# ViT layers on one core: in each MLP pair the transpositions move behind the first output tile, on DVE the normalised rows come first, on POOL the deviation comes ahead of the bias

## The reference

```python
for i in range(DEPTH):                      # DEPTH 4, DIM 128, HID 256, HEADS 8
    y = layernorm(h, ln1_w[i], ln1_b[i])
    ...                                     # attention
    h = h + (o @ proj_w[i] + proj_b[i])
    y = layernorm(h, ln2_w[i], ln2_b[i])
    y = jax.nn.gelu(y @ fc1_w[i] + fc1_b[i], approximate=False)
    h = h + (y @ fc2_w[i] + fc2_b[i])
```

## Time and profile before

| | us |
|---|---|
| median of 3 runs | 4164.19 |
| the profiled execution | 4193.22 |
| its span, which the profile shows | 4191.4 |
| mean granted TensorE clock | 0.943 of full speed |
| PE busy | 3591.3 (86%) |
| DVE, ACT, POOL busy | 2534.1, 1868.7, 2256.9 |
| time of PE's idle before L502, put down to the copy L605 | 58.5 |

### The profile page before, as it was taken

The page is one execution under the profiler, slowest core; times in us unless marked ns, Lnnn a source line. Parts: engine busy times, 40 slices in busy tenths (PEclk is TensorE's granted clock), DMA queues, the critical chain, the costliest instruction groups (busy, mean ns, idle before and its releaser), DMA issues. The chain is left out here.

```text
span 4191.4 us, 92430 instructions
## 1 busy us (share of the span) xinstructions
PE 3591.3 (86%) x30906; PEld 2764.9 (66%) x30906; DVE 2534.1 (60%) x6578; ACT 1868.7 (45%) x3340; POOL 2256.9 (54%) x2633
## 2 busy tenths in 40 slices
PE   8779999879999879999878999886887887876973
PEld 8757777667777657777656777763333665655763
DVE  1246776557776546777546777555775887865211
ACT  0036666336666435666534666542332443311331
POOL 0065663566664466666365666354554663264776
PEclk9879999999999989999998999998999998997997
DMA  6556664036666025666114666300000223131342
GB/s 222 162 106 122 126 127 92 3 72 127 125 125 117 8 53 109 123 126 127 37 36 89 122 126 125 72 1 28 22 22 20 57 64 48 35 87 41 65 63 29
DMA packets 456034, 341.81 MB, mean 82 GB/s; under 512 B 70659, under 2 KB 440171, under 8 KB 455595
## 3 DMA queue, kind: packets, MB, share of 16 engines
q1 hardware_dynamic: 413635, 314.62, 36.4%
q0 software_dynamic: 27136, 16.42, 2.9%
q10 hardware_dynamic: 15008, 7.51, 0.7%
HBM read 227.69 MB, written 109.29 MB: 80 GB/s over the span
## 5 line engine op out<-in xcount | busy, mean ns | idle before, releaser
L720 DVE TENSOR_REDUCE a_neg_max<-a_S 99x4 f32<-99x788 f32 x1024 | 1003.7, 980 | 560.3 <-PE a_S L351 546.5
L533 ACT ACTIVATE a_probs<-a_St 99x792 f32<-99x792 f32 (+1 forms) x1024 | 850.3, 830 | 683.5 <-PE a_St L368 671.9
L368 PE MATMUL a_St<-a_q_st,a_k_st 99*99 99x198 bf16 (+1 forms) x4096 | 530.1, 252 | 84.4 <-DMA a_q_st<-a_max_rows 70.2
L351 PE MATMUL a_S<-a_k_st,a_q_st 96*99 96x197 bf16 x4096 | 551.9, 258 | 45.7 <-DVE a_neg_max L720 45.5
L351 PEld LDWEIGHTS a_S<-a_k_st,a_q_st 96*99 96x99 bf16 x4096 | 399.5, 128 | 266.8 <-DVE a_neg_max L720 221.5
L368 PEld LDWEIGHTS a_St<-a_q_st,a_k_st 99*99 99x99 bf16 (+1 forms) x4096 | 391.5, 126 | 116.7 <-DMA a_q_st<-a_max_rows 69.6
L385 PE MATMUL a_O<-a_probs,a_v_aug 99*32 99x198 f32 (+1 forms) x8192 | 464.5, 339 | 0.4
L663 POOL TENSOR_TENSOR h<-h,a_rows 99x512 f32<-99x512 f32 x128 | 162.5, 1270 | 277.3 <-DVE a_m_xn L801 277.3
L385 PEld LDWEIGHTS a_O<-a_probs,a_v_aug 99*32 99x32 f32 (+1 forms) x8192 | 246.6, 110 | 84.7 <-issue 2.1
L631 POOL CAST a_max_parts<-a_neg_max 99x32 bf16<-99x32 f32 x128 | 26.8, 209 | 471.8 <-DVE a_neg_max L720 471.8
L512 PEld LDWEIGHTS a_O<-a_w,a_gelu 128*99 128x99 f32 x2048 | 241.7, 168 | 45.5 <-issue 29.2
(11 more groups left out here) (267 smaller groups left out, 7473.8 us busy)
## 6 DMA issues: line engine op xcount, KB each, us to landing
xpatch<-in_x SPq DMA_DIRECT2D x64, 594.0 KB, 3.7
spill_q<-a_parts SPq DMA_DIRECT2D x384, 99.0 KB
spill_k<-a_parts SPq DMA_DIRECT2D x384, 99.0 KB
a_k_st<-spill_k SPq DMA_DIRECT2D x128, 297.0 KB
a_q_st<-spill_q SPq DMA_DIRECT2D x128, 297.0 KB
a_k_st<-spill_k SPq DMA_DIRECT2D x128, 198.0 KB
a_q_st<-spill_q SPq DMA_DIRECT2D x128, 198.0 KB
a_k_st<-spill_k SPq DMA_DIRECT2D x128, 99.0 KB
```

The costliest lines, as they stand in the source:

```text
L351: mm = nc.tensor.matmul(S[0:TC, j // 2, j % 2 * TB:j % 2 * TB + NTOK], q_st[p % 4][0:SPLIT, head, b * TB + c * TC:b * TB + (c + 1) * TC], ...
L368: mm = nc.tensor.matmul(St[0:keys, j // 2, j % 2 * TB:(j % 2 + 1) * TB], k_st[p][:, head, first:first + keys], q_st[p][:, head, b * TB:(b ...
L533: nc.scalar.activation(probs[0:keys, u % 4, :].rearrange("p (x t) -> p x t", x=2), St[0:keys, :, 0:2 * TB], ACT.Exp).then_inc(s["probs"], 1)
L720: nc.vector.tensor_reduce(out.rearrange("p (x y) -> p x y", x=2), S[0:TC, :, 0:2 * TB].rearrange("p x (y t) -> p x y t", y=2)[:, :, :, 0:N ...
```

## The change

PE: the second layer's four output tiles get a helper `down(t)`; the first tile is issued, then the transpositions of pair k + 2, then the other three tiles. DVE: normalised rows (k + 2) are made ahead of the statistics (k + 3). POOL: the deviation (k + 3) is made ahead of the bias (k + 2). No instruction is added or dropped and no wait changes its value.

```diff
@@ tensor, mlp
+                    def down(t):
+                        for h in range(2):
+                            mm = nc.tensor.matmul(O[0:TC, t * D:(t + 1) * D], gl[k % 2][:, h, t * TC:(t + 1) * TC],
+                                                  m.w2[:, h * D:(h + 1) * D], start=(h == 0), stop=(h == 1))
+                        return mm
...
                         wait(pe, s["m_gelu"], 2 * (n + 1))
                         wait(pe, s["m_h"], n)
-                        for t in range(4):
-                            for h in range(2):
-                                mm = nc.tensor.matmul(O[0:TC, t * D:(t + 1) * D], gl[n % 2][:, h, t * TC:(t + 1) * TC],
-                                                      m.w2[:, h * D:(h + 1) * D], start=(h == 0), stop=(h == 1))
-                        mm.then_inc(s["m_fc2"], 1)
+                        down(0)
                     if 0 <= k + 2 < PAIRS:
...
                         mm.then_inc(s["m_turned"], 1)
+                    if 0 <= k < PAIRS:
+                        for t in range(1, 3):
+                            down(t)
+                        down(3).then_inc(s["m_fc2"], 1)
@@ gpsimd, mlp: this block moves from the head of the function to its end
-                    if 0 <= k + 2 < PAIRS:
-                        n = at(l, k + 2)
-                        wait(pool, s["m_xn"], n + 1)
-                        hp = g.h[0:TC, (k + 2) * 4:(k + 3) * 4, :]
-                        nc.gpsimd.tensor_tensor(hp, hp, m.b2.unsqueeze(1).to_broadcast([TC, 4, D]),
-                                                ALU.add).then_inc(s["m_bias"], 1)
@@ vector, mlp: this block moves from the head of the function to behind m_xn
-                    if 0 <= k + 3 < PAIRS:
-                        n = at(l, k + 3)
-                        q = n % 2
-                        wait(dve, s["h_done"], n + 1)
-                        wait(dve, s["m_aggr"], n - 1)
-                        for t in range(4):
-                            op = nc.vector.bn_stats(m_stats[q][:, t, :], g.h[0:TC, (k + 3) * 4 + t, :])
-                        op.then_inc(s["m_stats"], 1)
```

More of the change, by code:

```diff
@@ L509, in mlp @@
                         wait(pe, s["m_h"], n)
-                        for t in range(4):
-                            for h in range(2):
-                                mm = nc.tensor.matmul(O[0:TC, t * D:(t + 1) * D], gl[n % 2][:, h, t * TC:(t + 1) * TC],
-                                                      m.w2[:, h * D:(h + 1) * D], start=(h == 0), stop=(h == 1))
-                        mm.then_inc(s["m_fc2"], 1)
+                        down(0)
                     if 0 <= k + 2 < PAIRS:
-                        n = at(l, k + 2)
-                        wait(pe, s["m_xn"], n + 1)
-                        wait(pe, s["m_yT"], n)
+                        n2 = at(l, k + 2)
+                        wait(pe, s["m_xn"], n2 + 1)
+                        wait(pe, s["m_yT"], n2)
                         wait(pe, s["yT"], at(l + 1, done + 6))
@@ L676, in mlp @@
                                                 ALU.pow).then_inc(s["m_rstd"], 1)
+                    if 0 <= k + 2 < PAIRS:
+                        n = at(l, k + 2)
+                        wait(pool, s["m_xn"], n + 1)
+                        hp = g.h[0:TC, (k + 2) * 4:(k + 3) * 4, :]
+                        nc.gpsimd.tensor_tensor(hp, hp, m.b2.unsqueeze(1).to_broadcast([TC, 4, D]),
+                                                ALU.add).then_inc(s["m_bias"], 1)
                 program(lambda l, k: None, attn, mlp, looped=False)(pool)
@@ L788, in mlp @@
                 def mlp(l, k, done):
+                    if 0 <= k + 2 < PAIRS:
+                        n = at(l, k + 2)
+                        wait(dve, s["m_rstd"], n + 1)
+                        wait(dve, s["m_turned"], n - 1)
+                        nc.vector.tensor_tensor(m_xn[n % 2][:], g.h[0:TC, (k + 2) * 4:(k + 3) * 4, :],
+                                                m_rstd[n % 2][:].to_broadcast([TC, 4, D]), ALU.mult).then_inc(s["m_xn"], 1)
                     if 0 <= k + 3 < PAIRS:
@@ L796, in mlp @@
                         op.then_inc(s["m_stats"], 1)
[L797 to L802, removed]
                     if 0 <= k + 3 < PAIRS:
```

3 lines of the change are left out of this document (1 added, 2 removed).

## The result

The change makes the kernel slower by half a per cent: 4196.1 us (median of 20 runs, 4182.7 to 4216.4) against 4178.1 us (20 runs, 4154.1 to 4194.3), a ratio of 1.0053 with a 95% interval of 1.0038 to 1.0069. The forecast was 4189.0 against 4164.2, +25 us; the medians lie 18 us apart, and the ratio says 16 to 29 us.

What follows compares the result with a forecast made beforehand. The prediction took PE, busy 86% of the span, as the bound. Layer 3 (+1), the other three layers (+21) and the clock (+3) gave +25 us on 4164: 4189 us, 0.6% slower, range 4140 to 4214.

Steps and rivals of the forecast that it cites:

- The plain pair: MLP pairs without an attention step: POOL's bias holds `m_xn`, so the period is 4.35 us against 4.28, 0.07 worse.
- X + 3.22: Plain pair: when POOL starts the bias, counted from X, the moment `m_xn` of a pair really begins (us).
- X + 3.28: Plain pair: earliest start of the next `m_xn` on DVE, counted from the real beginning of this pair's `m_xn` (us).
- an instruction that slips in first: Plain pairs: DVE's `m_xn` gets ahead of POOL's bias and is not held; pairs take 3.53, total 4117 us; chance 0.12.
- the mixture: Plain pairs: `m_xn` is held by the bias in some pairs only; total 4135 to 4165 us; chance 0.06.
- The upper bound: Plain pair with nothing else late: PE alone takes 1.43 + 1.75 + 0.35 = 3.53 us, 0.75 less than now.
- Layer 3 and the first 13 intervals: Layer 3's 30 intervals: +1 us; layers 0 to 2 up to their first attention step: +0.8 us a layer.
- The wait in the steps: Attention steps: the bias ahead of `xn` makes PE wait longer, 4.4 us idle instead of 2.5; +2.6 four times a layer.
- The clock: Behind the attention steps: nine of twelve already show a clock fall, the other three fall too, about 1 us each: +3.
- From step to step: Between attention steps, some loss returns: behind k = 21 the cycle takes 25.25 us, today 23.6, so +1.7, not +2.6.
- The sum: Whole kernel: 1 for layer 3, 21 for the three other layers, 3 for the clock, together +25 us.
- The slower rival: Twelve attention steps cost 1.6 us more each (second clock fall 1.2, L616 held 0.44): 4209 us; chance 0.14.

Runs made afterwards that it cites:

- e5: Changed kernel with POOL's bias replaced by a memset of a scratch tile of about the same length, output bias left out; 4136.4 us (1 run).
- e6: Changed kernel with POOL's bias replaced by the same tensor_tensor on scratch tiles, output bias left out; 4203.4 us (1 run).
- e8: Changed kernel with POOL's bias split into two instructions of two row blocks each; 4179.7 us (1 run).
- e1: Changed kernel with only POOL's order undone (bias ahead of deviation again), PE and DVE as changed; 4107.7 us (5 runs), ratio 0.9861 to the original.
- e11: Original kernel with POOL making the attention step's xn ahead of pair k's bias and deviation; 4122.4 us (6 runs), ratio 0.9903 to the original.
- e12: Changed kernel with POOL making the attention step's xn ahead of pair k's deviation and bias; 4132.9 us (1 run).
- e10: e1 with POOL also making the attention step's xn ahead of pair k's bias and deviation; 4066.5 us (5 runs), ratio 0.9784 to the original.
- e7: Changed kernel with POOL's bias moved behind the attention step's xn, in the steps behind k = 13, 17, 21, 25, 29 only; 4205.8 us (1 run).
- e4: Original kernel with DVE's and POOL's new orders only, PE's order as before; 4179.0 us (1 run).

## Why the prediction was right, and where it was off

**The plain pair.** Forecast 4.35, measured 4.36. `m_xn` starts 0.06 behind the bias, as worked out from X + 3.22 and X + 3.28, and ends where the bias's shown end less 0.14 lets it: 2772.43 + 1.27 - 0.14 + 0.67 = 2774.23, measured 2774.24. e5, e6 and e8 show the mechanism, e1 its price. The rival of an instruction that slips in first falls, and so does the mixture. (That rival's price has a slip: 3 x (-16 + 6) is -30 and not -28, which makes it 4115; nothing hangs on it.) By the Trainium skill (SBUF — State Buffer, section "Who interferes with whom") a DVE instruction with two SBUF inputs contends with a GpSimd instruction that reads SBUF and not with one that only writes it, and the issue order decides who blocks; e5 and e6 agree with that, with 0.68 beside a memset and 1.76 beside a reader.

**The upper bound.** I had 3.53 for PE alone; e1 shows 3.42. What was off is the 1.43 from first to second layer, read where PE had just been idle. With no idle time ahead, the second layer starts 1.33 behind (2771.65 to 2772.98, and 1.33 in e1 too, 29 of the 30 times in layer 3; the one that follows a wait is 1.43). So the harm of POOL's order was larger than I said: 0.94 a pair and not 0.82.

**Layer 3 and the first 13 intervals.** Forecast +1 and +0.8; measured +1.3, and +0.7 in each layer (59.24 to 59.91 from the first layer of pair 0 to that of pair 14).

**The wait in the steps.** Forecast: transpositions of `xn` 8.76 behind the last first layer, 4.4 idle; measured 8.83 and 4.31. Over twelve steps the forecast +1.9 each is 22.8, and the rows give 51.7 - 30.2 = 21.5. The steps are the larger part of the loss, as forecast. PE's account of the MLP stages bears it out: its idle time rose by 25.1 (119.9 to 145.0), 21.5 of it ahead of the transpositions of `xn`, and its busy time by 4.8. Removing the wait on both sides (e11, e12) takes only 12 of the 30 us away, because a part of it comes back ahead of the transpositions of `m_xn`, in the changed order alone.

**The clock.** This is the term that was mis-sized: 3 us taken, about 10 found. Stretches of 8 us from the step's resumption on, before the change, behind k = 17 and 21 of layer 0 and the same two of layer 1 (columns as before):

```profile
831.54:839.54 8.00, 7.17 (x22) 4.23 (x23) 0.78 (x5) 2.27 (x4) 6.35 (x5) 0.59 0.11 28
856.07:864.07 8.00, 6.58 (x40) 4.81 (x40) 0.98 (x6) 2.87 (x5) 7.39 (x6) 1.00 0.17 48
1487.43:1495.43 8.00, 6.58 (x35) 4.57 (x36) 2.25 (x10) 2.81 (x6) 7.10 (x6) 1.00 0.15 41
1509.92:1517.92 8.00, 6.58 (x19) 3.92 (x20) 0.78 (x5) 1.69 (x3) 6.97 (x6) 0.54 0.14 38
```

After the change, behind k = 21 of layer 0:

```profile
856.09:864.09 8.00, 6.58 (x18) 4.11 (x19) 0.00 (x0) 1.69 (x3) 5.91 (x5) 0.50 0.11 29
```

1.00 is the upper level (2.4 GHz), 0.50 the lower (1.2 GHz). Before, nine of the twelve steps behind k = 13 to 25 show a fall, after all twelve, as forecast. But before has, without any change of order, the same stretch with and without a fall, and that gives the price. From the first layer of pair 18 to that of pair 22 it took 24.53, 22.47 and 24.63 in layers 0, 1 and 2, the 22.47 being the one at 1.00: 2.1 a fall. From pair 22 to pair 26 it took 23.45, 27.67 and 23.45, the 27.67 being the one at 0.54: 4.2 a fall. In after the three steps that were spared fall too: 4.2 + 2.1 + 4.2 = 10.5, an estimate at the prices of before. PE's busy time gives the same size for all falls together: in layers 0 to 2 it rose from 551.0 - 113.3 = 437.7 to 555.9 - 111.9 = 444.0 (+6.3), while in layer 3, where nothing falls, the new order took 1.5 off it; 6.3 + 3 x 1.5 = 10.8. I had multiplied a mean clock over 4 us and taken about 1 us; at 0.50 over 8 us it is 4, and the work under it is on the path. Whether the fall is tied to PE's idle time was argued in the prediction and is shown by the steps without it: of the twelve rows of 8 us, twelve are at 1.00 in e12, eleven in e11 and ten in e10 (the rest 0.79, 0.78 and 0.76), none in e1, which still idles 39.9 in all. In the 8 us behind these, all twelve are at 1.00 in e11, and five are below it in e12 and in e10 each, where PE has new waits of up to 4.4 us for `m_xn`; e11 has none of these.

**From step to step.** By the prediction behind k = 21 the next step resumes 25.25 later; it is 28.19 (856.09 to 884.28). The 23.6 that it started from is a cycle of before without a fall (856.07 to 879.53 is 23.46). The rows of after say where the other 2.9 are. The first layer comes 7.18 behind the resumption (863.27) and not 4.53, with PE at the lower clock: 2.65. The three pairs behind it take 4.56, 3.42 and 4.20 (to 875.45), 12.18 together, where the forecast comes to 11.96, and the wait ends 8.83 behind the last first layer, where it had 8.76. So this fall costs 2.7 and not the 4.2 of the same length of fall in before. There the first layer came 2.0 later (1509.92 to 1516.49, 6.57) and the pair behind it took 2.2 more; in after that pair was to wait for `m_xn` by the forecast, and what PE lost by the clock went into this wait.

| first layer to first layer, layers 0, 1, 2 | before | after |
|---|---|---|
| pair 0 to 14 | 59.24, 59.24, 59.24 | 59.91, 59.90, 59.91 |
| 14 to 18 | 22.53, 22.54, 22.54 | 24.05, 24.79, 23.97 |
| 18 to 22 | 24.53, 22.47, 24.63 | 26.46, 26.62, 26.41 |
| 22 to 26 | 23.45, 27.67, 23.45 | 28.19, 28.49, 28.18 |
| 26 to 30 | 31.10, 31.31, 31.16 | 31.42, 31.57, 31.41 |
| 30 to 31 | 17.42, 18.38, 18.38 | 18.56, 19.47, 18.58 |

**The sum.** Forecast 1 + 21 + 3 = 25. Measured in the MLP stages of the two profiled executions: 1.3 in layer 3, 2.0 in the first 14 intervals of the three others, 10.5 for the falls by the working above, and 16.1 left for the steps (forecast 3 x 6.2 = 18.6): 29.9. The step term was a little too large and the clock term too small by more; how the 26.6 split between these two is an estimate, since the falls are priced as in before. The medians are 18 apart, and the forecast of 25 was set against the medians. In how many executions of before a fall is spared is known for the profiled one alone, and I leave the 12 us between the two figures open.

**The slower rival** had the steps cost more than their wait: a second fall (1.2) and L616 held by `m_xn` (0.44). Its falls are there at a higher price than the rival had, but in three more steps and not in twelve; its hold is not there in after, where `xn` shows 1.04 as it does alone, and is there in e7 (1.40), where the order makes the two meet.

## What to carry to other kernels

When two engines wait for the same moment, look at what each has queued behind it: here a GpSimd `tensor_tensor` released by its own predecessor started 0.06 us ahead of a VectorE one released by a semaphore from that same predecessor, and since both read two operands of SBUF, the second waited out nearly the whole of the first (until 0.14 before its shown end). So an instruction that nobody needs soon belongs behind the one that everyone waits for: tie it to that one's end (e1), split it (e8), or let it write only. And where an engine that is not the bound feeds the one that is at the head of a stage, make that input ahead of the work of the stage before: e10 took 3.3 us of wait out of each step (39.9 / 12) and with it about half of the time at the lower clock in layers 0 to 2 (133 to 63 us). Then look where the wait has moved to: 19 us of it came back ahead of `m_xn` (2.3 to 21.4).

## What the runs showed that I had not expected

- PE's first layer to second layer is 1.33 when PE comes from work and 1.43 when it comes from a wait, with the same instructions: durations read behind an idle time are not those of a busy stretch.
- A fall of the granted clock behind a wait of 2.5 us costs 2.1 to 4.2 us of a cycle, and in before it comes in nine of twelve steps; with the wait gone the clock stayed at its upper level in 33 of 36 stretches of 8 us (e10, e11, e12), and fell in 10 of the 36 stretches behind these, only in the two kernels where PE waits for `m_xn` there.
- A producer's loop slower than its consumer (4.36 against 4.28) stayed out of sight for 22 pairs in e4. The same in a shorter stage would have looked like no effect.
- A POOL memset of 1,408 numbers a partition takes 1.27 us and leaves a DVE `tensor_tensor` beside it at 0.68.
